# Five of nine down products of a mixture-of-experts slot go over to transposed, split products

## The chip, the cores and the metric

One core of a Trainium2 chip runs the whole program. The metric is the device time of one execution in microseconds (us), from the first to the last instruction with what lies around it; of several executions the median is taken.

## The reference

The input x is 16 batches of 512 tokens with 128 features, in float32. Six residual blocks run over it. The first three belong to the half of the program that the change touches (the front), the others to the back.

```
x = x + 0.5 * moe(layernorm(x));  x = x + attn0(layernorm(x));  x = x + 0.5 * moe(layernorm(x))
x = x + 0.5 * mlp(x normalised);  x = x + softmax_attention(x); x = x + 0.5 * mlp(...)

moe:  scores = sigmoid(x @ gate.T); top 2 of 16 experts, weights divided by their sum -> comb
      ye[e] = (silu(x @ We_gate[e]) * (x @ We_up[e])) @ We_down[e]     (16 experts, inner size 64)
      y = sum_e comb[:, e] * ye[e]  +  (silu(x @ Ws_gate) * (x @ Ws_up)) @ Ws_down  (inner size 128)
```

## The kernel before

The program has three parts one after another: `build_weights` (loads and splits the weights), `build_front`, `build_back`. The front works through **slots**. A slot is one `moe` of one batch (main work) with a share of other work beside it (side work): `SIDE = [ATT, MLP, ATT, MLP]`, so ATT slots carry the linear attention of another batch and MLP slots an `mlp`. There are 34 slots: one with no side work first, then 8 turns of 4, then one with no side work that also starts the back's first batch (`first_batch`). Each slot also prepares the next slot's input (`PREPARE` gives the tile index at which each step of this stands).

The 16 experts are taken in pairs, so a slot has NT = 9 tiles of 128 inner rows: tile 0 is the shared expert, 1 to 8 are pairs. For tile n, all with 512 tokens (T = 4 groups of 128):

- TensorE, `gate`: G = gate product, and U = up product. `product` makes a float32 product out of three passes with fp32r operands split in a high and a low part (wh*high + wl*high + wh*low), each pass one matmul of 512 columns.
- TensorE, `routing_weights`: C = comb weights spread over the rows of the tile, one matmul.
- ScalarE: s = silu(G) (L537).
- VectorE, `activated`: su = U * s (L691), and `routed`: h = C * su (L700), in three buffers h[n % 3].
- TensorE, `moe_down` with `down` (L861): Y[tokens, features] += h[:, t].T @ wd[n], four plain float32 matmuls of 128 columns. The trace records each of them twice, hence "x8".

At the end `main_residual` (VectorE, L704) adds 0.5 * Y to x.

Each engine has a program of its own, written out by hand in the order in which it runs; the engines meet through counting semaphores (`Signal`). TensorE's order within a slot, tile n: gate n, up n, C n, side work, main transposes (`PREPARE["transpose"]`), router logits, then `moe_down(n - 1)`. After tile 8 it runs the next slot's gate 0, and then `moe_down(8)`. G has two banks in PSUM, so gate n waits for the silu of tile n - 2. 

Side work on TensorE in an ATT slot: transposes of the side input zs (tile 2), `kvu_product` (tiles 3 and 4), `queries` (4), `keys_values` (5), `attend` (6). In an MLP slot: `out_transposes` (0), `wout` product (1), transposes (2), `hidden` (3 to 6), `mlp_down` (5 to 8).

GpSimd (POOL) runs, slot by slot: `side_start` (scale and offset of the side layernorm, and xb = x + bias), `main_normalise` (z of the next slot), and in ATT slots sin and cos products (kc, qc), uw and ub, `scale_offset` of the output norm, then og. It can't read PSUM. In the last slot it normalises the back's first batch (L463 to L475, result e_xn), which TensorE transposes at tile 4 (L958).

Of the kernel before, what the change touches and what calls it, by code (L numbers as in the profile page):

```python
# [19 lines left out]
F32R = mybir.dt.float32r  # L20
# [11 lines left out]
I_E = 64  # L32
TE = E * I_E // P
NT = TE + 1
FT = 4
GRP = 4
HG = H // GRP
# [19 lines left out]
class Chain:  # L57
# [36 lines left out]


PREPARE = {
    MLP: {"statistics": 2, "transpose": 4, "low": 4, "logits": 5, "scores": 6, "best": 6, "next": 7, "weights": 8},
    ATT: {"statistics": 1, "transpose": 3, "low": 3, "logits": 4, "scores": 5, "best": 6, "next": 7, "weights": 8},
}

# [71 lines left out]
def build_front(nc, weights, early, x_dram, mid_dram, ident_dram, staged_dram, tail_dram, turns):  # L172
    w = weights
    with ExitStack() as ctx:
# [50 lines left out]
        sbuf_s = [sb(f"s{p}", [P, T, P]) for p in range(2)]  # L225
        su = [sb(f"su{k}", [P, T, P]) for k in range(2)]
        h = [sb(f"h{k}", [P, T, P]) for k in range(3)]

        kvu = sb("kvu", [P, T, 3 * D])
        kc = sb("kc", [P, 2, T, D])  # L230
# [13 lines left out]

        hs = [sb(f"hs{k}", [P, T, P]) for k in range(2)]

        G = [ps(f"G{k}", [P, T, P]) for k in range(2)]
        U = ps("U", [P, T, P])
        C = ps("C", [P, T, P])
        Y = ps("Y", [P, T, P])  # L250
# [24 lines left out]
        weight_ready = sig("weight_ready", TE * NM, TE)  # L275
        h_ready = sig("h_ready", TE * NM, TE)
        down_done = sig("down_done", NT * NM, NT)

        main_done = sig("main_done", NM, 2)
        side_done = sig("side_done", NM, 1)  # L280
# [110 lines left out]
        def _(pool):  # L391
# [20 lines left out]
            def main_normalise(q, i):  # L412
# [5 lines left out]
                own.settle()  # L418
                nc.gpsimd.tensor_tensor(z[:], z[:], rstd[:].broadcast_to([P, T, D]), ALU.mult).then_inc(z_ready.sem, 1)

            def side_start(m, i, k):
                scale_offset(rstd_s, off_s, vpe_s, mv_s, smv_ready, smv_ready.at(i, k + 1), srstd_ready)

                pool.wait_ge(side_done.sem, side_done.at(i, k))
                bias = w["bout"] if SIDE[m] == ATT else w["b2h"]
                nc.gpsimd.tensor_tensor(xb[:], xw[SIDE_BATCH[m]][:], bias[:], ALU.add).then_inc(xb_ready.sem, 1)

            main_normalise(-1, 0)
            main_normalise(0, 0)

            own.step(nc.gpsimd.memset(early.va[:], 0.0))
            own.settle()
# [3 lines left out]
            for i in range(turns):  # L436
                for m in range(NM):
                    side_start(m, i, m)
                    main_normalise(m + 1, i)
                    if SIDE[m] == ATT:  # L440
                        a = nth(m)

                        pool.wait_ge(ka_ready.sem, ka_ready.at(i, a + 1))
                        nc.gpsimd.tensor_tensor(kc[:, 1], kvu[:, :, 0:D], w["sin_t"][:],
                                                ALU.mult).then_inc(ks_ready.sem, 1)

                        pool.wait_ge(qa_ready.sem, qa_ready.at(i, a + 1))
                        own.step(nc.gpsimd.tensor_tensor(qc[:, 0], qa[:], w["cos_c"][:], ALU.mult))
                        nc.gpsimd.tensor_tensor(qc[:, 1], qa[:], w["sin_c"][:], ALU.mult).then_inc(qc_ready.sem, 1)

                        pool.wait_ge(kvu_out.sem, kvu_out.at(i, T * (a + 1)))
                        own.step(nc.gpsimd.tensor_tensor(uw[:], kvu[:, :, 2 * D:], w["lnw"][:], ALU.mult))
                        own.step(nc.gpsimd.tensor_tensor(ub[:], kvu[:, :, 2 * D:], w["lnb"][:], ALU.mult))
                        scale_offset(rstd2, off2, vpe2, mv2, mv2_ready, mv2_ready.at(i, a + 1), rstd2_ready)

                        pool.wait_ge(on_ready.sem, on_ready.at(i, a + 1))
                        own.step(nc.gpsimd.tensor_tensor(og[:], on[:], uw[:], ALU.mult))
                        own.settle()
                        nc.gpsimd.tensor_tensor(og[:], og[:], ub[:], ALU.add).then_inc(og_ready.sem, 1)

            pool.wait_ge(early.mv_ready.sem, 1)
            _, mv_e, ve_e, rs_e = early.norm
            own.step(nc.gpsimd.tensor_tensor(ve_e[:], mv_e[:, :, 1], w["eps_two"][:], ALU.add))  # L463
# [9 lines left out]
            own.step(nc.gpsimd.tensor_tensor(early.xn[:], og[:], w["lns"][:], ALU.mult))  # L473
            own.settle()
            nc.gpsimd.tensor_tensor(early.xn[:], early.xn[:], w["lnsb"][:], ALU.add).then_inc(early.xn_ready.sem, 1)  # L475

        @block.scalar
        def _(act):
# [36 lines left out]
            def first_batch(n):  # L515
# [8 lines left out]
                if n == 8:  # L524
                    act.wait_ge(first_v.sem, 1)
                    nc.scalar.activation(store_values(early.va), values_in(Z), ACT.Copy)

            def slot(m, i, side, prepare):
                g0, steps = NT * m, PREPARE[side or MLP]
                for n in range(NT):  # L530
                    act.wait_ge(gate_ready.sem, gate_ready.at(i, g0 + n + 1))
                    if n >= 2:
                        act.wait_ge(up_used.sem, up_used.at(i, g0 + n - 1))
                    elif n == 0 and up_used.at(i, g0) > 0:

                        act.wait_ge(up_used.sem, up_used.at(i, g0))
                    nc.scalar.activation(sbuf_s[n % 2][:], G[n % 2][:], ACT.Silu).then_inc(act_done.sem, 1)  # L537
                    if n == 0:
                        act.wait_ge(combT_ready.sem, combT_ready.at(i, m + 1))
                        nc.scalar.activation(cT[m % 2][:], Z[:], ACT.Copy).then_inc(cT_ready.sem, 1)  # L540
                    if n == 0 and side == MLP:
                        act.wait_ge(oT_mm.sem, oT_mm.at(i, nth(m - 1) + 1))
                        nc.scalar.activation(oT[:], S[0][:], ACT.Copy).then_inc(oT_ready.sem, 1)
                    if n == 1 and side:
                        side_normalise(m, i, m)
                    if n == 2 and side:
                        side_high(i, m)
                    if prepare and n == steps["logits"] + 1:
                        scores(m + 1, i)
                    if side == ATT:  # L550
                        a = nth(m)
                        if n == 4:
                            act.wait_ge(kvu_out.sem, kvu_out.at(i, T * (a + 1)))
                            nc.scalar.activation(kvu[:, :, 0:D], kvu[:, :, 0:D], ACT.Silu).then_inc(ka_ready.sem, 1)
                            act.wait_ge(q_mm.sem, q_mm.at(i, a + 1))
                            nc.scalar.activation(qa[:], S[1][:], ACT.Silu, bias=w["bq"][:]).then_inc(qa_ready.sem, 1)
                        if n == 7:
                            out_normalise(a, i)
                    elif side == MLP:
                        if 3 <= n < 3 + FT:  # L560
                            hidden(m, n - 3, i)
                    if prepare:
                        if n == steps["transpose"]:
                            main_high(m + 1, i)
                        if n == steps["logits"]:
                            logits_half(m + 1, i)
                    else:
                        first_batch(n)

            main_high(-1, 0)  # L570
            logits_half(-1, 0)
# [8 lines left out]
        def _(dve):  # L580
# [112 lines left out]
            def routed(m, n, i):  # L693
# [1 line left out]
                g0, c0 = NT * m, TE * m  # L695
                dve.wait_ge(up_used.sem, up_used.at(i, g0 + n + 1))
                dve.wait_ge(weight_ready.sem, weight_ready.at(i, c0 + n))
                if n >= 3:
                    dve.wait_ge(down_done.sem, down_done.at(i, g0 + n - 2))
                nc.vector.tensor_tensor(h[n % 3][:], C[:], su[n % 2][:], ALU.mult).then_inc(h_ready.sem, 1)  # L700

# [130 lines left out]
        def _(pe):  # L832
# [30 lines left out]
                return mm  # L863

            def moe_down(m, n, i):
                if n == 0:

                    pe.wait_ge(main_done.sem, main_done.at(i, m))
                    pe.wait_ge(up_used.sem, up_used.at(i, NT * m + 1))
                else:  # L870
                    pe.wait_ge(h_ready.sem, h_ready.at(i, TE * m + n))
                down(Y, h[n % 3], w["wd"][:, n], n == 0).then_inc(down_done.sem, 1)

            def comb_transposes(m, i):
                if m < 0:
# [95 lines left out]

            def gate(m, n, i):
                g0 = NT * m
                if n >= 2:
                    pe.wait_ge(act_done.sem, act_done.at(i, g0 + n - 1))
                elif n == 0:
                    pe.wait_ge(xl_ready.sem, xl_ready.at(i, m + 1))
                    if m >= 0:

                        pe.wait_ge(act_done.sem, act_done.at(i, g0))  # L980
                product(G[n % 2], w["wgh"][:, n], w["wgl"][:, n], xh[m % 2], xl[m % 2]).then_inc(gate_ready.sem, 1)

            def slot(m, i, side, prepare):
                g0, a, steps = NT * m, nth(m), PREPARE[side or MLP]
                high, low = xh[m % 2], xl[m % 2]
                for n in range(NT):
# [34 lines left out]
                        logits(m + 1, i)  # L1021
                    if not prepare:
                        first_batch(n)
                    if n >= 1:
                        moe_down(m, n - 1, i)
                    if side == ATT:
                        if n == 2:
                            side_transposes(i, m)
# [3 lines left out]
                            keys_values(a, i)  # L1032
                if prepare:
                    gate(m + 1, 0, i)
                moe_down(m, NT - 1, i)

            main_transposes(-1, 0)
# [641 lines left out]
def build_weights(nc, front, back, a):  # L1679
# [24 lines left out]
    for name, (shape, _) in plain.items():  # L1704
        sb(name, shape)
    sb("wd", [P, NT, D])
    for name in ("minus_half", "eps", "eps_two", "both"):
        sb(name, [P, T])
    parts = {
# [18 lines left out]
    with ExitStack() as tmp:  # L1728
# [105 lines left out]
        def _(act):  # L1834
# [3 lines left out]
            for k, (whole, high, _) in enumerate(halves):  # L1838
                if k == first_others:
                    wait_loads(act, "others")  # L1840
                nc.scalar.activation(high, whole, ACT.Copy).then_inc(high_ready, 1)
            for n, f in enumerate(angle):
                act.wait_ge(angle_ready, n + 1)
                nc.scalar.activation(w[f + "_t"][:], angle[f][:], ACT.Sin).then_inc(table_ready, 1)
# [88 lines left out]
```

## Time and profile before

| | us |
|---|---|
| median of 3 runs | 1971.51 (1969.16 to 1973.76) |
| the profiled execution | 1970.83 |
| its span, first to last instruction | 1969.0 |
| TensorE busy in the span | 1879.2 (95%) |
| VectorE, ScalarE, GpSimd busy | 1533.5, 1167.0, 669.0 |

The front lasts to about 1146 us, with some 24 us of preparation ahead of it. "Busy" counts the time in which an instruction of the engine runs. Matmuls overlap each other in the records, so their cost is read from the distance between two starts, not from their length. In a timeline, a bracket at the end of a row is the engine's idle time before it and what ended that.

### The profile page before, as it was taken

The numbers are of one execution on the slowest core, as the hardware profiler recorded it, in microseconds if no ns is written. First come the engines' busy times: TensorE is split into PE (matmuls) and PEld (weight loads), VectorE is DVE, ScalarE is ACT, GpSimd is POOL, SyncE is SP. The second block draws the span as 40 slices with busy tenths as digits, with TensorE's granted clock in tenths as the row PEclk, the third lists the DMA queues.
The fourth block names the chain that finished last, engine by engine and source line by source line (L and its number), as shares of the span: only waits on it lengthen the run. The fifth ranks groups of instructions, "written<-read, shape, count | busy, mean of one in ns | idle before, by whom it ended". The sixth has DMA issues, their size and how long they took to land. (4 is left out here: it accounts for less than half of the span.)

```text
span 1969.0 us, 34154 instructions
## 1 busy us (share of the span) xinstructions
PE 1879.2 (95%) x12340; PEld 1296.4 (66%) x12340; DVE 1533.5 (78%) x3824; ACT 1167.0 (59%) x2178; POOL 669.0 (34%) x768
## 2 busy tenths in 40 slices
PE   2999999999999999999999989999999999999996
PEld 2888888888888888888888844444444444444433
DVE  5776767676767776777677669999999999999991
ACT  2444444444444444444444328888888888888885
POOL 2333433343334333433343323333333333333311
PEclk9999999999999999999999969999999999999998
DMA  3000000000000000000010022222222222222210
GB/s 133 7 12 1 12 11 12 1 12 12 11 1 11 12 12 1 12 12 11 1 38 6 6 86 87 87 87 87 90 94 91 91 92 92 92 88 87 86 46 11
DMA packets 49991, 85.81 MB, mean 44 GB/s; under 512 B 6752, under 2 KB 11104, under 8 KB 49760
## 3 DMA queue, kind: packets, MB, share of 16 engines
q1 hardware_dynamic: 47920, 81.85, 13.0%
q8 instruction: 99, 1.62, 0.3%
q10 hardware_dynamic: 1904, 1.78, 0.3%
q14 instruction: 68, 0.56, 0.1%
HBM read 49.26 MB, written 34.87 MB: 43 GB/s over the span
## 5 line engine op out<-in xcount | busy, mean ns | idle before, releaser
L1528 DVE TENSOR_REDUCE b_nm<-b_MX 128x1 f32<-128x512 f32 x1024 | 648.6, 682 | 46.0 <-PE b_MX L1636 31.2
L1420 ACT ACTIVATE b_pr<-b_ST 128x512 f32<-128x512 f32 x1024 | 550.2, 603 | 101.0 <-PE b_ST L1624 96.7
L537 ACT ACTIVATE s<-G 128x512 f32<-128x512 f32 x306 | 182.6, 597 | 294.6 <-PE G L856 290.3
L691 DVE TENSOR_TENSOR su<-U,s 128x512 f32<-128x512 f32 x272 | 187.0, 687 | 208.7 <-PE U L856 106.4
L861 PE MATMUL Y<-w_wd,h 128*128 128x128 f32 x2448 | 328.2, 277 | 4.3 <-DVE h L700 4.3
L861 PEld LDWEIGHTS Y<-w_wd,h 128*128 128x128 f32 x2448 | 308.8, 192 | 26.7 <-DVE h L700 14.7
L1636 PE MATMUL b_MX<-b_kt,b_qt 32*128 32x512 f32 x768 | 240.6, 504 | 2.2 <-DVE b_nm L1528 1.8
L1624 PE MATMUL b_ST<-b_qt,b_kt 32*128 32x512 f32 x768 | 213.9, 494 | 6.1 <-ACT b_pr L1420 6.1
L1624 PEld LDWEIGHTS b_ST<-b_qt,b_kt 32*128 32x128 f32 x768 | 83.3, 181 | 203.8 <-ACT b_pr L1420 135.9
L700 DVE TENSOR_TENSOR h<-C,su 128x512 f32<-128x512 f32 x272 | 188.0, 691 | 9.3
L854 PE MATMUL G<-xh,w_wgh 128*128 128x512 f32 x306 | 145.5, 475 | 0.0
L404 POOL TENSOR_TENSOR vpe_s<-mv_s,w_eps 128x4 f32<-128x4 f32 x32 | 6.4, 200 | 399.6 <-DVE mv_s L595 399.6
L1651 PE MATMUL b_PV<-b_pr,e_va 128*32 128x512 f32 x1024 | 139.0, 615 | 0.0
L1651 PE MATMUL b_PV<-b_pr,b_va 128*32 128x512 f32 x1024 | 136.4, 605 | 0.0
L854 PE MATMUL U<-xh,w_wuh 128*128 128x512 f32 x306 | 126.7, 414 | 1.2 <-DVE h L691 0.7
L856 PE MATMUL G<-xl,w_wgh 128*128 128x512 f32 x306 | 121.2, 396 | 0.0
L855 PE MATMUL G<-xh,w_wgl 128*128 128x512 f32 x306 | 121.0, 396 | 0.0
L856 PE MATMUL U<-xl,w_wuh 128*128 128x512 f32 x306 | 120.8, 395 | 0.0
L855 PE MATMUL U<-xh,w_wul 128*128 128x512 f32 x306 | 120.0, 392 | 0.0
L889 PE MATMUL C<-cT,w_pairs 128*128 128x512 f32 x272 | 107.7, 396 | 0.0
L1636 PEld LDWEIGHTS b_MX<-b_kt,b_qt 32*128 32x128 f32 x768 | 95.9, 185 | 15.9 <-DVE b_nm L1528 11.5
L494 ACT ACTIVATE zs<-xw,off_s,rstd_s 128x128 f32<-128x128 f32 x128 | 52.8, 483 | 66.6 <-POOL off_s L410 66.6
(295 smaller groups left out, 3629.7 us busy)
## 6 DMA issues: line engine op xcount, KB each, us to landing
b_kt<-staging SPq DMA_DIRECT2D x48, 256.0 KB, 2.7
b_qt<-staging SPq DMA_DIRECT2D x48, 256.0 KB, 3.0
staging<-e_khi SPq DMA_DIRECT2D x32, 256.0 KB, 2.9
staging<-e_qhi SPq DMA_DIRECT2D x32, 256.0 KB, 3.1
xin<-in_x SPq DMA_DIRECT2D x17, 256.0 KB, 2.8
mid<-xo SPq DMA_DIRECT2D x16, 256.0 KB, 2.0
staging<-e_klo SPq DMA_DIRECT2D x16, 256.0 KB, 3.0
staging<-e_qlo SPq DMA_DIRECT2D x16, 256.0 KB, 3.0
```

Of the source, the lines that this page charges most:

```text
L537: nc.scalar.activation(sbuf_s[n % 2][:], G[n % 2][:], ACT.Silu).then_inc(act_done.sem, 1)
L691: nc.vector.tensor_tensor(out[:], U[:], sbuf_s[n % 2][:], ALU.mult).then_inc(up_used.sem, 1)
L700: nc.vector.tensor_tensor(h[n % 3][:], C[:], su[n % 2][:], ALU.mult).then_inc(h_ready.sem, 1)
L854: pe.matmul(flat(bank), wh, flat(high), start=True, stop=False)
L855: pe.matmul(flat(bank), wl, flat(high), start=False, stop=False)
L856: return pe.matmul(flat(bank), wh, flat(low), start=False, stop=True)
L861: mm = pe.matmul(bank[:, t], hid[:, t], wd, start=(first and t == 0), stop=True, skip_group_check=True)
L1420: nc.scalar.activation(pr[k % 2][:, j], bank[:].rearrange("p a b -> p (a b)"), ACT.Exp, scale=SM_SCALE).then_inc(used["st"].sem, 1)
L1528: nc.vector.tensor_reduce(nm[g % 2][:, c:c + 1], bank[:].rearrange("p a b -> p (a b)"), AX.X, ALU.max).then_inc(used["mx"].sem, 1)
L1624: pe.matmul(flat(bank_of(B, "st", 0, u)), kt_[g][rows_of(j), k % T], flat(qt[g])[rows_of(j)], start=True, stop=True).then_inc(made["st"].s ...
L1636: pe.matmul(flat(bank_of(B, "mx", rel, u)), qt[g][rows_of(j), u // HG % T], flat(kt_[g])[rows_of(j)], start=True, stop=True).then_inc(made ...
L1651: mm = pe.matmul(flat(PV)[rows_of(j)], values_of(va[B.parity], kt, g, j), pr[k % 2][:, j], start=(k % (PAIR * T) == 0), stop=((k + 1) % (P ...
```

## The change

Tiles 2 to 6 (`V0, NV = 2, 5`) of each slot get another down product. ScalarE copies h to hh (fp32r, the high part), GpSimd makes hl = h - hh (the low part), and TensorE adds three passes of 512 columns, wdh*hh + wdl*hh + wdh*hl, to a bank V that holds the sum transposed (features x tokens). At the end of the slot ScalarE copies V to vs and TensorE adds its transposes to Y. V takes the place of the second G bank, so gate n now waits for the silu of tile n - 1. The down products of tiles 2 to 6 stand one tile later on TensorE (`moe_down(n - 2)`), so tile 3 has none, and tile 8 has those of tiles 6 and 7. The main statistics in MLP slots go from tile 2 to tile 1, GpSimd's xb goes behind `main_normalise`, and the weights wdh and wdl are made once.

```diff
+V0, NV = 2, 5
 PREPARE = {
-    MLP: {"statistics": 2, "transpose": 4, ...
+    MLP: {"statistics": 1, "transpose": 4, ...
...
+        hh = [sb(f"hh{k}", [P, T, P], F32R) for k in range(3)]
+        hl = [sb(f"hl{k}", [P, T, P], F32R) for k in range(3)]
+        vs = sb("vs", [P, T, P])
-        G = [ps(f"G{k}", [P, T, P]) for k in range(2)]
+        G = ps("G", [P, T, P])
+        V = ps("V", [P, T, P])
...  GpSimd
+            def low(m, n, i):
+                pool.wait_ge(hh_ready.sem, hh_ready.at(i, NV * m + n - V0 + 1))
+                nc.gpsimd.tensor_tensor(hl[n % 3][:], h[n % 3][:], hh[n % 3][:],
+                                        ALU.subtract).then_inc(hl_ready.sem, 1)
...
             main_normalise(-1, 0)
+            own.step(nc.gpsimd.tensor_tensor(w["wdl"][:], w["wd"][:, V0:V0 + NV], w["wdh"][:], ALU.subtract))
+            own.settle()
             main_normalise(0, 0)
+            lows(-1, 0, range(V0, V0 + NV))
...
                     side_start(m, i, m)
-                    main_normalise(m + 1, i)
-                    if SIDE[m] == ATT:
+                    if SIDE[m] == MLP:
+                        main_normalise(m + 1, i)
+                        lows(m, i, (2,))
+                        side_bias(m, i, m)
+                        lows(m, i, (3, 4, 5, 6))
+                    else:
                         a = nth(m)
+                        main_normalise(m + 1, i)
+                        lows(m, i, (2,))
+                        side_bias(m, i, m)
+                        lows(m, i, (3,))
...  (kc, then qc)
+                        lows(m, i, (4,))
...  (uw, ub)
+                        lows(m, i, (5,))
                         scale_offset(rstd2, off2, vpe2, mv2, mv2_ready, mv2_ready.at(i, a + 1), rstd2_ready)
+                        lows(m, i, (6,))
...  (og)
+            lows(0, turns, (2, 3))
             pool.wait_ge(early.mv_ready.sem, 1)
...  (e_xn)
+            lows(0, turns, (4, 5, 6))
...  ScalarE
+            def high(m, n, i):
+                act.wait_ge(h_ready.sem, h_ready.at(i, TE * m + n))
+                nc.scalar.activation(hh[n % 3][:], h[n % 3][:], ACT.Copy).then_inc(hh_ready.sem, 1)
+            def down_copy(m, i):
+                act.wait_ge(down_done.sem, down_done.at(i, NT * m + V0 + NV))
+                nc.scalar.activation(vs[:], V[:], ACT.Copy).then_inc(vs_ready.sem, 1)
...  (slot, behind the silu of tile n; down_copy at the slot's end)
+                    if V0 < n <= V0 + NV:
+                        high(m, n - 1, i)
...  VectorE, routed
-                if n >= 3:
+                if n >= V0 + 3:
+                    dve.wait_ge(hl_ready.sem, hl_ready.at(i, NV * m + n - V0 - 2))
+                elif n >= 3:
                     dve.wait_ge(down_done.sem, down_done.at(i, g0 + n - 2))
...  TensorE, moe_down
+                k = n - V0
+                if 0 <= k < NV:
+                    high, low = hh[n % 3], hl[n % 3]
+                    pe.wait_ge(hh_ready.sem, hh_ready.at(i, NV * m + k + 1))
+                    pe.matmul(flat(V), w["wdh"][:, k], flat(high), start=(k == 0), stop=False, skip_group_check=True)
+                    pe.wait_ge(hl_ready.sem, hl_ready.at(i, NV * m + k + 1))
+                    pe.matmul(flat(V), w["wdl"][:, k], flat(high), start=False, stop=False, skip_group_check=True)
+                    pe.matmul(flat(V), w["wdh"][:, k], flat(low), start=False, stop=True,
+                              skip_group_check=True).then_inc(down_done.sem, 1)
+                    return
...
+            def down_transposes(m, i):
+                pe.wait_ge(vs_ready.sem, vs_ready.at(i, m + 1))
+                for t in range(T):
+                    pe.matmul(Y[:, t], vs[:, t], w["ident"][:], start=False, stop=True, is_transpose=True,
+                              skip_group_check=True)
...  gate
-                if n >= 2:
-                    pe.wait_ge(act_done.sem, act_done.at(i, g0 + n - 1))
+                if n >= 1:
+                    pe.wait_ge(act_done.sem, act_done.at(i, g0 + n))
...  slot
-                    if n >= 1:
+                    if 1 <= n <= V0:
                         moe_down(m, n - 1, i)
+                    if n >= V0 + 2:
+                        moe_down(m, n - 2, i)
+                    if n == NT - 1:
+                        moe_down(m, NT - 2, i)
...
                 if prepare:
                     gate(m + 1, 0, i)
+                down_transposes(m, i)
                 moe_down(m, NT - 1, i)
...  build_weights, ScalarE, ahead of the sine tables
+            wait_loads(act, "down")
+            nc.scalar.activation(w["wdh"][:], w["wd"][:, V0:V0 + NV], ACT.Copy)
```

## Rows read from the trace of the kernel before

**Rows 1.** Busy time by engine in two stretches: start:end, length, engines, granted clock, DMA.
```profile
300.00:500.00 200.00, 197.28 (x1257) 172.16 (x1256) 144.68 (x434) 89.47 (x156) 70.48 (x89) 1.00 0.03 9
1148.00:1150.00 2.00, 0.80 (x3) 0.29 (x3) 0.00 (x0) 0.00 (x0) 1.86 (x4) 0.50 0.82 255
```

**Rows 2.** Timeline of TensorE, ATT slot: start us, length us, engine, line, operation, tiles.
```profile
409.07 0.60 PE L839 MATMUL Z<-w_ident,z 128*128 128x128 f32 x4
409.51 1.06 PE L861 MATMUL Y<-w_wd,h 128*128 128x128 f32 x8
410.32 0.48 PE L854 MATMUL G<-xh,w_wgh 128*128 128x512 f32 x1
...
411.10 0.40 PE L854 MATMUL U<-xh,w_wuh 128*128 128x512 f32 x1
...
411.79 0.40 PE L889 MATMUL C<-cT,w_pairs 128*128 128x512 f32 x1
...
413.88 1.14 PE L861 MATMUL Y<-w_wd,h 128*128 128x128 f32 x8
414.77 0.48 PE L854 MATMUL S<-xhs,w_wqh 128*128 128x512 f32 x1
...
421.46 1.95 PE L944 MATMUL S<-kvm,qc 128*128 128x128 f32 x16
...
430.25 1.16 PE L861 MATMUL Y<-w_wd,h 128*128 128x128 f32 x8 [0.22 <-DVE h L700]
...
431.16 0.48 PE L854 MATMUL U<-xh,w_wuh 128*128 128x512 f32 x1
```

**Rows 3.** Timeline of TensorE, the MLP slot that follows.
```profile
445.38 0.66 PE L839 MATMUL Z<-w_ident,z 128*128 128x128 f32 x4 [0.22 <-POOL z L419]
...
459.21 0.48 PE L854 MATMUL G<-xh,w_wgh 128*128 128x512 f32 x1
...
464.22 0.47 PE L854 MATMUL U<-xh,w_wuh 128*128 128x512 f32 x1
```

**Rows 4.** Timeline of TensorE, the first and the last slot of the front.
```profile
56.36 0.66 PE L839 MATMUL Z<-w_ident,z 128*128 128x128 f32 x4 [1.13 <-POOL z L419]
...
1130.12 0.60 PE L958 MATMUL Z<-w_ident,e_xn 128*128 128x128 f32 x4
...
1149.03 0.80 PE L1636 MATMUL b_MX<-e_kt,e_qt 32*128 32x512 f32 x3 [3.01 <-DMA e_qt<-staging]
```

**Rows 5.** Timeline of ScalarE: preparation, ATT slot, MLP slot.
```profile
21.14 0.63 ACT L1844 ACTIVATE w_cos_t<-t_angle_cos 128x512 f32<-128x512 f32 x1 [5.26 <-DVE t_angle_cos L1826]
...
405.24 0.57 ACT L537 ACTIVATE s<-G 128x512 f32<-128x512 f32 x1
...
418.35 0.26 ACT L490 ACTIVATE en<-lg 128x64 f32<-128x64 f32 x1
...
426.75 1.51 ACT L494 ACTIVATE on<-S,off,rstd 128x128 f32<-128x128 f32 x4 [1.12 <-POOL off L410]
...
457.20 0.60 ACT L537 ACTIVATE s<-G 128x512 f32<-128x512 f32 x1
```

**Rows 6.** Timeline of GpSimd: ATT slot, then last slot of the front.
```profile
415.14 1.80 POOL L444 TENSOR_TENSOR kc<-kvu,w_sin_t 128x512 f32<-128x512 f32 x1 [6.72 <-ACT kvu L554]
...
424.83 0.20 POOL L404 TENSOR_TENSOR vpe<-mv,w_eps 128x4 f32<-128x4 f32 x1 [2.92 <-DVE mv L595]
...
429.69 1.27 POOL L459 TENSOR_TENSOR og<-og,ub 128x512 f32<-128x512 f32 x1
...
1120.99 0.20 POOL L463 TENSOR_TENSOR e_ve<-e_mv,w_eps_two 128x4 f32<-128x4 f32 x1 [21.11 <-DVE e_mv L595]
...
1126.23 1.30 POOL L475 TENSOR_TENSOR e_xn<-e_xn,w_lnsb 128x512 f32<-128x512 f32 x1
```

**Rows 7.** Timeline of VectorE, ATT slot.
```profile
418.64 0.82 DVE L628 TENSOR_SCALAR en<-en 128x64 f32<-128x64 f32 x1
...
430.11 0.93 DVE L669 TENSOR_TENSOR first<-first,second 128x64 f32<-128x64 f32 x1
```

More of the change, by code:

```diff
@@ L96 @@
 PREPARE = {
-    MLP: {"statistics": 2, "transpose": 4, "low": 4, "logits": 5, "scores": 6, "best": 6, "next": 7, "weights": 8},
+    MLP: {"statistics": 1, "transpose": 4, "low": 4, "logits": 5, "scores": 6, "best": 6, "next": 7, "weights": 8},
     ATT: {"statistics": 1, "transpose": 3, "low": 3, "logits": 4, "scores": 5, "best": 6, "next": 7, "weights": 8},
@@ L277, in build_front @@
         down_done = sig("down_done", NT * NM, NT)
+        hh_ready = sig("hh_ready", NV * NM, NV)
+        hl_ready = sig("hl_ready", NV * NM, NV)
+        vs_ready = sig("vs_ready", NM, 1)
         main_done = sig("main_done", NM, 2)
@@ L419, in main_normalise, with lows, side_bias @@
                 nc.gpsimd.tensor_tensor(z[:], z[:], rstd[:].broadcast_to([P, T, D]), ALU.mult).then_inc(z_ready.sem, 1)
+            def low(m, n, i):
+                pool.wait_ge(hh_ready.sem, hh_ready.at(i, NV * m + n - V0 + 1))
+                nc.gpsimd.tensor_tensor(hl[n % 3][:], h[n % 3][:], hh[n % 3][:],
+                                        ALU.subtract).then_inc(hl_ready.sem, 1)
+            def lows(m, i, tiles):
+                for n in tiles:
+                    low(m, n, i)
             def side_start(m, i, k):
                 scale_offset(rstd_s, off_s, vpe_s, mv_s, smv_ready, smv_ready.at(i, k + 1), srstd_ready)
+            def side_bias(m, i, k):
                 pool.wait_ge(side_done.sem, side_done.at(i, k))
@@ L536, in slot @@
                         act.wait_ge(up_used.sem, up_used.at(i, g0))
-                    nc.scalar.activation(sbuf_s[n % 2][:], G[n % 2][:], ACT.Silu).then_inc(act_done.sem, 1)
+                    nc.scalar.activation(sbuf_s[n % 2][:], G[:], ACT.Silu).then_inc(act_done.sem, 1)
                     if n == 0:
@@ L568, in slot @@
                         first_batch(n)
+                down_copy(m, i)
             main_high(-1, 0)
@@ L973, in gate @@
                 g0 = NT * m
[L974 to L976 removed]
+                if n >= 1:
+                    pe.wait_ge(act_done.sem, act_done.at(i, g0 + n))
+                else:
                     pe.wait_ge(xl_ready.sem, xl_ready.at(i, m + 1))
@@ L980, in gate @@
                         pe.wait_ge(act_done.sem, act_done.at(i, g0))
-                product(G[n % 2], w["wgh"][:, n], w["wgl"][:, n], xh[m % 2], xl[m % 2]).then_inc(gate_ready.sem, 1)
+                product(G, w["wgh"][:, n], w["wgl"][:, n], xh[m % 2], xl[m % 2]).then_inc(gate_ready.sem, 1)
             def slot(m, i, side, prepare):
@@ L1706, in build_weights @@
     sb("wd", [P, NT, D])
+    sb("wdh", [P, NV, D], F32R)
+    sb("wdl", [P, NV, D], F32R)
     for name in ("minus_half", "eps", "eps_two", "both"):
```

## The prediction

> **What bounds the kernel now.** I looked first at the busy time in stretches. In the middle of the front TensorE is busy for 197 of 200 us, with the clock granted in full; VectorE has 145, ScalarE 89, GpSimd 70 [rows 1]. So work taken off TensorE counts nearly in full, as long as the slower engines keep up. Next the timeline of TensorE, where costs are distances between starts. An old down product takes 0.81 (409.51 to 410.32), and the gate pass behind it starts a product of 0.78 (410.32 to 411.10) where the up product of the same form takes 0.69 (411.10 to 411.79). So the change from float32 to fp32r costs 0.08 or 0.09, and a down costs 0.89 all told, as in 413.88 to 414.77 [rows 2]. A three-pass product is what the new down will be: 0.70. Four transposes cost 0.44 (409.07 to 409.51) [rows 2]. Last, the brackets: in the slots shown TensorE waits 0.22 for h of tile 8 at 430.25 and 0.22 for z at 445.38, and in the first slot 1.13 for z [rows 2 to 4].
>
> **The change, TensorE's work.** Each slot loses five downs of 0.89, and 0.08 more at tile 4 of ATT (tile 5 of MLP), where the down stands between two fp32r groups: 4.53. It gains five products of 0.70 and one group of transposes, 3.50 + 0.44 = 3.94. That is 0.59 a slot less, 20 us over 34 slots.
>
> **ATT slots.** I follow the trace of before with only the changed steps moved. Tile 3 has no down, and the later products are shorter, so TensorE could reach `attend` 1.25 earlier than 421.46: 0.89 from tile 3, 0.27 at tile 4, and 0.19 at tile 5, less some 0.1 that the wait for xls ahead takes. ScalarE however must do high(4) (0.60, as any copy of 128x512; a silu is 0.57 to 0.60 [rows 5]) ahead of the table load for the router scores, so en comes at 418.1 instead of 418.35, only 0.25 earlier. VectorE runs four score steps behind en and then the mask of the heads that `attend` needs, and one of them is likely held by a GpSimd operation, below. I get the mask at 420.4 and `attend` at 420.5: 0.95 early, a new wait of 0.3.
> From the end of `attend` to the next slot's up product TensorE now needs 7.9 (431.16 less 421.46 + 1.78). After: product 4 0.78, two times gate, up and C 3.26, products 5 and 6 1.40, the down of tile 7 0.81, gate 0 0.78, transposes 0.44, the down of tile 8 0.89, sum 8.4; the down that no longer stands at tile 3 comes back here, and the wait of 0.22 goes. Product 6 needs GpSimd's low(6), which stands behind `scale_offset`. That begins at 424.83 and hands over at 426.7, where ScalarE's `on` starts [rows 5, 6]. Both come 0.8 earlier, at 425.9; low(6) costs 1.3 (og, a product of the same size, is 1.27 [rows 6]) and ends at 427.2, and TensorE asks at 427.2 to 427.3. I charge 0.1. The gain of an ATT slot is 0.95 - 0.5, about 0.5.
>
> **MLP slots.** GpSimd has nothing but z, xb and the low parts, and each low part is there a microsecond or more ahead of its product. The statistics at tile 1 fall into VectorE's idle time while ScalarE waits for the side norm, z comes 3 us earlier, and the wait of 0.22 goes. Gate 8 needs the silu of tile 7 (457.20), which stands behind high(5) and two table loads; I get 456.4 for it and 457.2 for gate 8 (before 459.21 [rows 3, 5]), a slack of 0.8. The product at the end waits for nothing. Gain 0.59 + 0.22, and 0.1 for places where two float32 groups come together: 0.9.
>
> **One bank for G.** Gate n is held by the silu of tile n - 1. The tightest place is gate 3 of ATT: silu 2 ends at 405.8 [rows 5] and gate 3 can start then, as before. A wait for xls stands behind it and hides a slip of 0.2. Cost 0, bound 0.4 a slot.
>
> **The ends.** First slot: 0.59 and the wait of 1.13 for z, 1.7. Preparation: the copy of wd stands ahead of the sine tables, where ScalarE later waits 5.26 for VectorE's cosine angles [rows 5], so 0; if the load were late it could cost 2. GpSimd makes wdl while it is idle.
> Last slot: here the change adds a wait that has no cover. GpSimd does low(2) and low(3) first and then normalises the back's first batch. That chain takes 6.5 (1120.99 to 1127.5 [rows 6]), and before it was over 2.6 ahead of its transposes at 1130.12 [rows 4]. Low(3) needs high(3), which needs silu 4 and with it gate 4, at the very tile where TensorE waits for the result. In the slot's old times: gate 4 ends at 1128.3, silu, high and low bring 1131.1, the chain 1137.6. TensorE stands from 1129.3 to 1137.7, and the transposes are 7.6 later than before. The keys and queries of the first batch, their staging and the back's first matmul (1149.03 [rows 4]) all hang on these transposes. After an idle time of 3 us the clock was granted at 0.50, the lower level, at the start of the back [rows 1, 4], so I add 2 for products at 1.2 GHz after the stall: 9.5 lost (bounds 7 and 12).
>
> **Sum.** 16 x 0.5 + 16 x 0.9 + 1.7 - 9.5 = 14.6. The profiled execution is 1970.8, which gives 1956.2; the median of the runs is 0.7 higher: 1957.
>
> **GpSimd and VectorE.** Two rows of before show that they hold each other up. VectorE's en + 1 takes 0.82 and its first + second 0.93, with GpSimd in a product of two SBUF tiles that ends at that moment (og runs from 429.69 to 430.96, first + second from 430.11 to 431.04); GpSimd's kc takes 1.80 instead of 1.27 beside VectorE's own kc product [rows 6, 7]. The low parts add five GpSimd operations of this kind to a slot, and about 20 small VectorE operations of the router lie among them.
> The Trainium skill ("SBUF — State Buffer", Who interferes with whom) says that an operation with two SBUF inputs on VectorE contends with a GpSimd instruction that reads SBUF, and that the second to issue fully blocks until the first has finished. The trace agrees, with the 0.93 above. By that rule every small operation that meets a low part waits up to 1.3; it is the rule that speaks most against the change, and rival D is what it could do.
>
> **Rivals.**
> B, all waits are covered: the mask and low(6) come in time, and an ATT slot gains its full 0.59 and the idle 0.3. For it: my two waits are each a few tenths and come out of small shifts. Against: both chains pass through two engines that are now busier. Price 16 x 0.4 = 6.4 better: 1950.
> C, the silu comes late: the single bank of G, with ScalarE's queue lengthened by five copies, holds a gate by 0.8 in each MLP slot beyond my slack (the place is gate 8 behind the two table loads). For it: silu 7 is the latest silu of before. Against: 0.8 of slack. Price 16 x 0.8 = 13: 1970.
> D, slower: low parts take 1.80 as kc does, since VectorE's two-input operations hold them. Three stand ahead of the output norm and product 6 in an ATT slot (4, 5 and 6), 0.5 each, so product 6 and the silu of tile 8 come 1.5 late: 16 x 1.5 = 24, 1981. It makes the kernel slower than before from 0.9 lost a slot (14.6 / 16). For it: the slack at product 6 is nil. Against: uw and ub run in the same stretch at about 1.3 undisturbed.
> That the new product is not cheaper than the old one is not among them, because gate and up have its exact form.
>
> **How the numbers follow.** About 0.2% (4 us) is what a measurement of this kernel can tell from no change. Chances: forecast (1952 to 1963) 0.50, B 0.17, C 0.20 (1963 to 1975, half of it faster by over 0.2%), D 0.13. Faster 0.77, same 0.10, slower 0.13. The range takes in B with some room, and C up to 1972; D and the rest stay out: 1946 to 1972.
>
> **What would show it.** Starts of new products 0.70 apart from what follows; in ATT slots TensorE waiting some tenths ahead of `attend` for VectorE (kvm) and hardly for hl; an idle TensorE of about 8.4 us ahead of the e_xn transposes in the last slot, with a granted clock of 0.50 behind it; slots in the middle shorter by 0.5 and 0.9. Wrong would be: brackets with hl or hh on many rows, brackets with s at gates, low parts of 1.8, or a last slot without the wait.

## The result, and the profile after

The changed kernel takes 1959.65 us (1958.95 to 1959.95, 4 runs) against 1971.69 of the kernel before, a ratio of 0.9939 with a 95% interval of 0.9922 to 0.9956. Forecast were 1957 and "faster". The profiled execution has a span of 1957.2.

From the page of the kernel after, the engines' busy times and the groups of the low and the high parts:

```profile
PE 1860.5 (95%) x11626; PEld 1258.0 (64%) x11626; DVE 1553.3 (79%) x3824; ACT 1272.9 (65%) x2383; POOL 886.6 (45%) x939
...
L432 POOL TENSOR_TENSOR hl<-h,hh 128x512 fp32r<-128x512 f32 x170 | 219.3, 1290 | 180.6 <-ACT hh L565 180.6
...
L565 ACT ACTIVATE hh<-h 128x512 fp32r<-128x512 f32 x170 | 105.9, 623 | 0.0
```

GpSimd's low part takes 1.29 on average over 170 of them (not the 1.8 of rival D), and ScalarE's high part 0.62. Ahead of the low parts GpSimd sat idle for 180 us in all, waiting for hh.

The busy times in the middle of the front, and then stretches of the last slot. The third figure from the end is the granted clock, as a share of the full one:

```profile
300.00:500.00 200.00, 197.42 (x1149) 168.42 (x1148) 150.27 (x433) 111.84 (x200) 113.86 (x124) 1.00 0.03 9
...
1112.00:1114.00 2.00, 0.00 (x0) 0.00 (x0) 0.00 (x0) 0.00 (x0) 1.92 (x2) 0.70 0.00 0
1116.00:1118.00 2.00, 2.00 (x8) 1.71 (x7) 0.53 (x1) 0.60 (x1) 0.00 (x0) 0.50 0.00 0
1118.00:1120.00 2.00, 2.00 (x7) 1.57 (x6) 0.17 (x1) 0.59 (x2) 0.00 (x0) 0.60 0.00 0
1120.00:1122.00 2.00, 2.00 (x11) 1.61 (x10) 1.38 (x2) 0.63 (x3) 1.29 (x1) 1.00 0.01 4
```

TensorE is as busy as before (197.4 of 200, [rows 1]); VectorE went from 145 to 150, ScalarE from 89 to 112, GpSimd from 70 to 114.

The best yardstick is the distance from one slot's first up product to the next one's. It is steady to some hundredths of a us within a kind of slot, so a single profile gives it. The means over 16 slots of a kind, with the first slot, the stretch from the last slot's up product to the back's first matmul, and the rest:

| | before | after | change | forecast |
|---|---|---|---|---|
| ATT slot | 32.40 | 32.33 | -0.07 | -0.5 |
| MLP slot | 33.05 | 31.83 | -1.22 | -0.9 |
| first slot | 34.26 | 32.21 | -2.05 | -1.7 |
| last slot, to the back | 30.29 | 38.91 | +8.62 | +9.5 |
| ahead of the first up product | 37.24 | 38.12 | +0.88 | 0 |
| back | 819.97 | 821.41 | +1.44 | 0 |

In sum 16 x (0.07 + 1.22) = 20.6 and 2.05 gained, 8.62 + 0.88 + 1.44 = 10.9 lost: 11.8, the difference of the spans. The last two lines are scatter. Over eleven profiles (both kernels and the nine experiments below) the preparation ends between 36.1 and 39.9, without order between kernels that share it, and the back lasts 818.3 to 822.1.

The total is 2.6 us from the forecast, but two terms of it were off by 7 and 5 us in opposite directions, and that they nearly cancelled was luck. So the experiments ask first where an ATT slot's gain went.

**An ATT slot after.** TensorE, the slot that starts at 391.18 and ends at 423.51:

```profile
391.18 0.48 PE L903 MATMUL U<-xh,w_wuh 128*128 128x512 f32 x1
...
412.75 2.02 PE L1010 MATMUL S<-kvm,qc 128*128 128x128 f32 x16
414.53 0.48 PE L919 MATMUL V<-hh,w_wdh 128*128 128x512 f32 x1
...
419.27 0.40 PE L919 MATMUL V<-hh,w_wdh 128*128 128x512 f32 x1
...
419.99 1.05 PE L910 MATMUL Y<-w_wd,h 128*128 128x128 f32 x8
...
421.58 0.60 PE L937 MATMUL Y<-w_ident,vs 128*128 128x128 f32 x4
422.60 1.16 PE L910 MATMUL Y<-w_wd,h 128*128 128x128 f32 x8 [0.41 <-DVE h L749]
423.51 0.48 PE L903 MATMUL U<-xh,w_wuh 128*128 128x512 f32 x1
```

`attend` stands 21.57 after the slot's start, and 22.70 in the slot of [rows 2] (421.46, its start being 431.16 less 32.40): 1.13 gained up to there. From the row behind `attend` to the end it takes 8.98 (414.53 to 423.51), and 7.92 before, from this row to 431.16:

```profile
423.24 1.06 PE L861 MATMUL Y<-w_wd,h 128*128 128x128 f32 x8
```

Product 6 (419.27 to 419.99) shows no wait for its low part. The transposes start at 421.58 and need 0.44, but the down of tile 8 starts at 422.60: 0.58 lost to h.

VectorE, GpSimd and ScalarE at that place:

```profile
417.90 0.69 DVE L749 TENSOR_TENSOR h<-C,su 128x512 f32<-128x512 f32 x1
418.51 0.93 DVE L699 TENSOR_TENSOR hit<-rest,m 128x64 f32<-128x64 f32 x1
...
419.99 1.09 DVE L710 TENSOR_TENSOR second<-hit,r 128x64 f32<-128x64 f32 x1
...
421.14 0.68 DVE L738 TENSOR_TENSOR su<-U,s 128x512 f32<-128x512 f32 x1
```

```profile
406.68 1.80 POOL L474 TENSOR_TENSOR kc<-kvu,w_sin_t 128x512 f32<-128x512 f32 x1 [1.36 <-ACT kvu L600]
...
418.06 1.29 POOL L432 TENSOR_TENSOR hl<-h,hh 128x512 fp32r<-128x512 f32 x1
419.72 1.28 POOL L490 TENSOR_TENSOR og<-on,uw 128x512 f32<-128x512 f32 x1 [0.36 <-ACT on L529]
```

```profile
410.21 0.26 ACT L525 ACTIVATE en<-lg 128x64 f32<-128x64 f32 x1
...
419.52 0.61 ACT L581 ACTIVATE s<-G 128x512 f32<-128x512 f32 x1
```

VectorE is done with h of tile 7 at 418.5 and goes on with the router's step `next`. Its first operation (L699) takes 0.93 instead of 0.22, and ends as low(6) ends (418.06 + 1.29 = 419.35). By then `next` is 0.7 late, and its `second` (L710) starts inside og, which began at 419.72: it takes 1.09, until og ends at 421.0. Only then comes su of tile 8, at 421.14, although s was there at 420.1. The rows of [rows 7] had one such hold in this place of the slot, on the step behind h of tile 8 (L669), where hardly anything waited for it.

**An MLP slot after.** TensorE, the transposes of z in the slot that starts at 1065.06:

```profile
1077.78 0.60 PE L888 MATMUL Z<-w_ident,z 128*128 128x128 f32 x4
```

They have no bracket any more, and stand 12.72 after the slot's start, against 14.22 in [rows 3] (445.38 less 431.16).

**The last slot after.** TensorE, then GpSimd:

```profile
1107.31 0.43 PE L955 MATMUL C<-cT,w_pairs 128*128 128x512 f32 x1
1115.69 1.11 PE L1024 MATMUL Z<-w_ident,e_xn 128*128 128x128 f32 x4 [7.96 <-POOL e_xn L509]
1116.46 0.78 PE L919 MATMUL V<-hh,w_wdh 128*128 128x512 f32 x1
...
1135.79 0.50 PE L1707 MATMUL b_MX<-e_kt,e_qt 32*128 32x512 f32 x3 [2.71 <-DMA e_qt<-staging]
```

```profile
1107.92 1.26 POOL L432 TENSOR_TENSOR hl<-h,hh 128x512 fp32r<-128x512 f32 x1 [0.43 <-ACT hh L565]
1109.14 0.20 POOL L497 TENSOR_TENSOR e_ve<-e_mv,w_eps_two 128x4 f32<-128x4 f32 x1
...
1114.38 1.26 POOL L509 TENSOR_TENSOR e_xn<-e_xn,w_lnsb 128x512 f32<-128x512 f32 x1
```

Low(3) runs from 1107.92 and the chain of the early norm right behind it, until 1115.64. TensorE waits 7.96. The transposes stand 18.81 after the last slot's up product (1096.88), 11.38 before: 7.43 late, where 7.6 were forecast. TensorE had stood idle since the C product of 1107.31. The granted clock was 0.70 in 1112:1114 (a mean of its upper level and the lower one, 1.2 GHz), 0.50 in 1116:1118, with TensorE at work again since 1115.69, and 1.00 from 1120 on. From the transposes to product 2 it takes 0.77 there (1115.69 to 1116.46), and 0.35 at full clock in `early_norm_first` below.

### The profile page after: what moved, and what is told of

Read it like the earlier page. It is cut to its first block and busy times, and to the rows that moved or that the text cites. A ratio compares the mean times of both kernels' runs of the same rounds, so it can differ in the third digit from the quotient of the medians.

```text
span 1957.2 us, 33103 instructions
## 1 busy us (share of the span) xinstructions
PE 1860.5 (95%) x11626; PEld 1258.0 (64%) x11626; DVE 1553.3 (79%) x3824; ACT 1272.9 (65%) x2383; POOL 886.6 (45%) x939
## 5 line engine op out<-in xcount | busy, mean ns | idle before, releaser
L432 POOL TENSOR_TENSOR hl<-h,hh 128x512 fp32r<-128x512 f32 x170 | 219.3, 1290 | 180.6 <-ACT hh L565 180.6
L910 PE MATMUL Y<-w_wd,h 128*128 128x128 f32 x1088 | 145.3, 276 | 6.7 <-DVE h L749 6.7
L910 PEld LDWEIGHTS Y<-w_wd,h 128*128 128x128 f32 x1088 | 137.7, 192 | 16.8 <-DVE h L749 10.5
L903 PE MATMUL G<-xh,w_wgh 128*128 128x512 f32 x306 | 136.0, 444 | 0.7 <-ACT s L581 0.7
L565 ACT ACTIVATE hh<-h 128x512 fp32r<-128x512 f32 x170 | 105.9, 623 | 0.0
```

The source lines that it names most:

```text
L432: nc.gpsimd.tensor_tensor(hl[n % 3][:], h[n % 3][:], hh[n % 3][:], ALU.subtract).then_inc(hl_ready.sem, 1)
L903: pe.matmul(flat(bank), wh, flat(high), start=True, stop=False)
L910: mm = pe.matmul(bank[:, t], hid[:, t], wd, start=(first and t == 0), stop=True, skip_group_check=True)
```

## The experiments

All edits are to the kernel after, if nothing else is said. "Slot" is the distance from above.

### early_norm_first: the back's norm ahead of the low parts

```diff
-            lows(0, turns, (2, 3))
             pool.wait_ge(early.mv_ready.sem, 1)
...
-            lows(0, turns, (4, 5, 6))
+            lows(0, turns, (2, 3, 4, 5, 6))
```

> The changed kernel with one move on GpSimd in the last slot of the front: the norm of the back's first batch (e_xn) runs ahead of low(2) and low(3). Theory: the wait of 7.96 us ahead of the e_xn transposes comes only from that order, and with the clock at half speed behind it the last slot lost 8.6 us; so the stretch from the last up product 0 to the back's first matmul falls from 38.9 to about 29.7 us (30.3 in the kernel before, less 0.6 of TensorE work), and the time to about 1950.5 us. Rival: ScalarE and GpSimd are too full in that slot whatever the order, and most of the wait comes back at product 2 or 3, waiting for hl; then the stretch stays above 34 us and the time above 1955.

Measured: 1949.13 us (1948.05 to 1951.02), ratio to the kernel before 0.9883 (0.9869 to 0.9898). The last stretch is 28.88 us, down from 38.91; slots as in after (32.32, 31.80). TensorE, last slot:

```profile
1107.98 0.43 PE L954 MATMUL C<-cT,w_pairs 128*128 128x512 f32 x1
1108.25 0.60 PE L1023 MATMUL Z<-w_ident,e_xn 128*128 128x128 f32 x4
1108.60 0.48 PE L918 MATMUL V<-hh,w_wdh 128*128 128x512 f32 x1
```

The transposes follow C at once and none of the later products waits. The order of GpSimd's program was the whole loss: it is worth 10.0 us in that stretch, 0.8 more than expected, since a wait of 0.45 for h of tile 8 in the kernel before (at 1144.86) is gone as well, and the wait for the DMA ahead of the back is 0.3 shorter.

### att_next_earlier: the router's `next` at tile 6

```diff
-    ATT: {..., "best": 6, "next": 7, "weights": 8},
+    ATT: {..., "best": 6, "next": 6, "weights": 8},
```

> The changed kernel with the router's step 'next' on VectorE in ATT slots one tile earlier (tile 6 instead of 7), where GpSimd runs only tiny operations. Theory: an ATT slot is 32.33 us long, 0.5 longer than its TensorE work, because VectorE's two-input operations there are held by GpSimd's low(6) (0.93 instead of 0.2) and then by og (1.09), so h of tile 8 comes 0.6 late (wait of 0.41 at the down of tile 8). Then the ATT slot falls to about 31.9 us, the wait at tile 8 goes, and the time falls by 6 us to about 1953.5. Rival: ScalarE's queue (high(6), then the output norm, then silu 8) sets h of tile 8; then VectorE waits for s instead, the slot stays at 32.3 and the time at 1959.5.

Measured: 1979.33 us (1977.25 to 1981.16), ratio to before 1.0039 (1.0024 to 1.0053): slower than both kernels. ATT slot 33.60, MLP slot 31.83. The theory and the rival both failed, and the trace says why. VectorE, GpSimd, and TensorE's wait:

```profile
422.96 0.23 DVE L710 TENSOR_TENSOR second<-hit,r 128x64 f32<-128x64 f32 x1
423.10 1.28 DVE L712 TENSOR_TENSOR share<-sc,den 128x64 f32<-128x64 f32 x1
424.31 0.68 DVE L738 TENSOR_TENSOR su<-U,s 128x512 f32<-128x512 f32 x1
```

```profile
423.01 1.29 POOL L432 TENSOR_TENSOR hl<-h,hh 128x512 fp32r<-128x512 f32 x1
```

```profile
425.05 0.49 PE L903 MATMUL U<-xh,w_wuh 128*128 128x512 f32 x1 [1.69 <-DVE su L738]
```

The step ran free of holds up to its last operation. That one (share, L712) started 0.09 behind low(6) and was held for the whole of it, 1.28 instead of 0.22, and behind it on VectorE stood su of tile 7, which frees U: TensorE waits 1.69 for it (26.8 us over the 16 slots). The place of a hold matters more than its number: in after, two holds of together 1.6 cost 0.58; here one of 1.1 made the slot 1.3 longer than in after.

### low6_memset: a low(6) that reads nothing

```diff
-                        lows(m, i, (6,))
+                        pool.wait_ge(hh_ready.sem, hh_ready.at(i, NV * m + 6 - V0 + 1))
+                        nc.gpsimd.memset(hl[0][:].bitcast(F32), 0.0).then_inc(hl_ready.sem, 1)
```

> The changed kernel with the low part of tile 6 in ATT slots left out: GpSimd fills hl with zeros instead (it writes SBUF and reads nothing), so the product of tile 6 lacks the share of its low part in these slots. Theory that GpSimd's reads hold VectorE: the hit step of 'next' takes 0.2 instead of 0.93, 'next' is over before og starts, so its 'second' step takes 0.2 instead of 1.09, the wait of 0.41 for h of tile 8 goes, and the ATT slot falls from 32.33 to about 31.75 us; time about 1950. Rival (ScalarE's queue sets h of tile 8): slot at 32.2 or more.

Measured: 1946.34 us in one run; ATT slot 31.60, MLP slot 31.82. VectorE, and GpSimd beside it:

```profile
416.10 0.21 DVE L700 TENSOR_TENSOR hit<-rest,m 128x64 f32<-128x64 f32 x1
...
416.86 0.23 DVE L711 TENSOR_TENSOR second<-hit,r 128x64 f32<-128x64 f32 x1
...
417.74 0.69 DVE L739 TENSOR_TENSOR su<-U,s 128x512 f32<-128x512 f32 x1 [0.52 <-ACT s L582]
```

```profile
415.62 0.53 POOL L488 MEMSET hl<- 128x512 f32 x1
417.31 1.28 POOL L491 TENSOR_TENSOR og<-on,uw 128x512 f32<-128x512 f32 x1 [1.16 <-ACT on L530]
```

`hit` takes 0.21 and `second` 0.23; `next` is over before og begins, and su of tile 8 waits for s, not for VectorE. The slot is 0.73 shorter: with low(6) both holds go. (The next one in line, on the step behind h of tile 8, comes back as it was before the change, at 0.95, and again hardly anything waits for it.) But the memset is also shorter than low(6), 0.53, and ends at 416.15, when `hit` had just begun. So this run doesn't tell whether the reading of low(6) holds VectorE or only its length. That needs a long operation that only writes.

### low6_memset_long: a second memset behind the first

```diff
                         nc.gpsimd.memset(hl[0][:].bitcast(F32), 0.0).then_inc(hl_ready.sem, 1)
+                        nc.gpsimd.memset(pad[:], 0.0)
```

(Against low6_memset; `pad` is 128x1024.)

> low6_memset with a second memset of GpSimd behind the first, of 128x1024 into a tile that nothing reads, so that GpSimd only writes from 415.6 to about 417.2 (estimate: 2 x 0.53 more). (As in low6_memset the low part of tile 6 is left out in ATT slots: zeros take its place.) VectorE's next step (hit to share, eight operations from 416.1 to 417.0) then lies wholly inside a GpSimd operation. Theory: VectorE is held by a GpSimd operation that reads SBUF, not by one that only writes: every operation of the step keeps its 0.15 to 0.23, and the ATT slot stays at 31.60 (31.5 to 31.7). Rival: any long GpSimd operation holds it, and low6_memset escaped because its memset ended 0.05 after hit had begun: second or one of the operations behind hit then takes about 1 us (until 417.2), the step ends 0.3 to 1 later, and the ATT slot is up to 0.4 longer, 31.7 to 32.0. In both MLP slot 31.82, total 1943 to 1950.

Measured: 1957.57 us in one run; ATT slot 32.18, MLP slot 31.81. Neither forecast had this. VectorE, and GpSimd beside it:

```profile
419.41 0.23 DVE L705 TENSOR_TENSOR hit<-hit,w_ramp 128x64 f32<-128x64 f32 x1
419.55 0.58 DVE L707 TENSOR_SCALAR den<-den 128x4 f32<-128x4 f32 x1
...
420.38 1.35 DVE L715 TENSOR_TENSOR share<-sc,den 128x64 f32<-128x64 f32 x1
421.65 0.68 DVE L741 TENSOR_TENSOR su<-U,s 128x512 f32<-128x512 f32 x1
```

```profile
419.15 0.95 POOL L490 MEMSET pad<- 128x1024 f32 x1
420.37 1.28 POOL L493 TENSOR_TENSOR og<-on,uw 128x512 f32<-128x512 f32 x1 [0.26 <-ACT on L532]
```

The 2-input operation L705 (`hit` times the ramp) lies wholly inside the memset and takes 0.23: not held, as my theory had it. But the tensor_scalar behind it (L707, 128x4, one input) is held until the memset ends, 0.58 instead of 0.16, in each of the 16 ATT slots. I had not told the two kinds apart. The Trainium skill does ("SBUF — State Buffer", Who interferes with whom): a VectorE instruction with two SBUF inputs contends with a GpSimd instruction that reads SBUF and not with one that only writes it, while a tensor_scalar can enter a 2-port mode, in which it contends with GpSimd. This trace agrees with both, by the 0.23 and the 0.58.

What follows is worth more. The hold of 0.42 alone should cost nothing, since VectorE waited 0.52 for s in low6_memset. But it made `share` (L715) start 0.01 behind og, which held it for 1.35, and su starts at 421.65. So the slot is 0.58 longer than in low6_memset, by a first hold of another cause than in the kernel after. A delay of some 0.4 that pushes `next` into og is all that it takes.

### stats_back_at_2: the early statistics undone

```diff
-    MLP: {"statistics": 1, ...
+    MLP: {"statistics": 2, ...
```

> The changed kernel with the main statistics in MLP slots and in the first slot back at tile 2. Theory: the MLP slot's gain of 1.22 us, more than the 0.59 of TensorE work plus the old wait of 0.22, leans on z being there early: TensorE now asks for z 1.3 us earlier than before, so at tile 2 the statistics cost a wait of about 1.3 us for z, and 0.5 more since low(2) stands behind z; MLP slot 31.83 to about 33.3 us, first slot 2 us longer, time about 1984. Rival: the early statistics only remove the old wait of 0.22; MLP slot about 32.1 us, time about 1965.

Measured: 1994.03 us in one run. MLP slot 33.78 (1.95 more than after), first slot 36.27, ATT slot 32.34. TensorE, an MLP slot:

```profile
449.36 0.66 PE L888 MATMUL Z<-w_ident,z 128*128 128x128 f32 x4 [1.13 <-POOL z L427]
...
450.59 0.50 PE L921 MATMUL V<-hh,w_wdl 128*128 128x512 f32 x1 [0.34 <-POOL hl L432]
```

The mechanism is the one forecast, z first and low(2) behind it, and it is larger: 2.0 a slot instead of 1.5, 4 instead of 2 in the first slot. (There the wait for z is 1.89, and the granted clock was 0.50 for some 3 us behind it.) Without this one digit the change would have made the kernel 22 us slower.

### before_one_bank: the kernel before with one bank for G

```diff
-        G = [ps(f"G{k}", [P, T, P]) for k in range(2)]
+        G = ps("G", [P, T, P])
...
-                if n >= 2:
-                    pe.wait_ge(act_done.sem, act_done.at(i, g0 + n - 1))
+                if n >= 1:
+                    pe.wait_ge(act_done.sem, act_done.at(i, g0 + n))
```

> The kernel before with the one bank for G alone (gate n waits for the silu of tile n - 1), nothing else changed. Theory: every silu is over before TensorE comes to the next gate, so both kinds of slot stay as long as before (ATT 32.40, MLP 33.05 us, within 0.05) and the time stays at 1971. Rival C of the prediction (the silu comes late, above all behind the two table loads): MLP or ATT slots 0.4 to 0.8 longer, time 1978 to 1984.

Measured: 1972.92 us in one run (before, on the same chip, 1973.1); slots 32.40, 33.04, first slot 34.28, each within 0.02 of the kernel before. The bank alone costs nothing. This run lacks the five high parts that lengthen ScalarE's queue; for these the trace of after has to answer (below, rival C).

### before_early_stats: the kernel before with the statistics at tile 1

```diff
-    MLP: {"statistics": 2, ...
+    MLP: {"statistics": 1, ...
```

> The kernel before with the main statistics of MLP slots and of the first slot at tile 1 instead of 2, nothing else changed. Theory: the gap of 0.38 us ahead of the z transposes goes in MLP slots (33.05 to 32.67 us) and 1.5 us in the first slot, time about 1963.5: about half a percent comes from this part without the new products. Rival: VectorE is late for something else at tile 1 and gives it back; MLP slot 33.0 or more, time 1970.

Measured: 1965.95 us in one run. MLP slot 32.62 (0.43 less), first slot 32.96 (1.30 less), ATT slot 32.40. The slots are near the theory; the time is 2.5 above it, as much as this profile's preparation (39.72) is longer than that of before. So 16 x 0.43 + 1.30 = 8.2 us of the change's gain come without any new product.

### att_four_tiles: early_norm_first, and no low(6) in ATT slots

```diff
+def tiles_v(m, i):
+    return NV - 1 if m >= 0 and SIDE[m] == ATT and i < NB // 2 else NV
...
-                        lows(m, i, (6,))
...
-                if 0 <= k < NV:
+                if 0 <= k < tiles_v(m, i):
```

(The counts of the semaphores follow, and the copy of V waits for tile 5 in these slots.)

> early_norm_first, and in ATT slots tile 6 keeps the old float32 down product, so GpSimd makes no low(6) there. Theory (GpSimd's reads hold VectorE's router step): TensorE does 0.19 us more in an ATT slot, but the wait for h of tile 8 and the delay that VectorE passes on go; ATT slot 32.32 to about 31.8 us, MLP slot 31.80 as in early_norm_first, time 1949 to about 1941. Rival (the zeros in low6_memset gained by being shorter, or by freeing TensorE of its wait for hl): ATT slot 32.3 or longer by the 0.19, time 1949 to 1952.

Measured: 1940.55 us (1939.53 to 1941.81), ratio to before 0.9839 (0.9823 to 0.9856). ATT slot 31.83, MLP slot 31.81. TensorE at the slot's end, and VectorE's `next`:

```profile
418.95 0.60 PE L945 MATMUL Y<-w_ident,vs 128*128 128x128 f32 x4
419.39 1.06 PE L918 MATMUL Y<-w_wd,h 128*128 128x128 f32 x8
```

```profile
415.70 0.22 DVE L707 TENSOR_TENSOR hit<-rest,m 128x64 f32<-128x64 f32 x1
...
416.46 0.23 DVE L718 TENSOR_TENSOR second<-hit,r 128x64 f32<-128x64 f32 x1
```

The down of tile 8 follows the transposes after 0.44: no wait. One new product less, and the slot is 0.49 shorter.

### all_four_tiles: early_norm_first with NV = 4

```diff
-V0, NV = 2, 5
+V0, NV = 2, 4
```

> early_norm_first with four new products in every slot (NV = 4, tiles 2 to 5) instead of five. Theory: ATT slot about 31.8 us as in att_four_tiles, MLP slot 31.80 plus the 0.19 that one old down costs over a new product, 31.99; time about 1944. Rival (each new product is worth more than 0.19 since the low part's path counts too, or less since its cover is nil): MLP slot outside 31.9 to 32.1.

Measured: 1943.08 us (1942.45 to 1946.26), ratio 0.9853 (0.9838 to 0.9868). ATT slot 31.81, MLP slot 32.01: 0.21 more than with five products. That is the price difference of one old and one new product, in slots that otherwise run alike; the prediction had 0.89 - 0.70 = 0.19. (Its first slot is 34.59 long, 1.8 more than in `att_four_tiles`. A GpSimd memset of 1.38 held VectorE's en + 1, a tensor_scalar, for 1.14, where it took 0.20 in `att_four_tiles`, and TensorE waited 1.31 instead of 0.35 for su. Behind that wait the granted clock was 0.50 in 66:68, and the two downs of tiles 6 and 7 took 3.07 there, 1.70 in the MLP slots.)

## Why the prediction was right, and where it was not

**TensorE's work** was right: 0.59 a slot rests on 0.19 for each product, where all_four_tiles shows 0.21, and on 0.44 for the transposes, which att_four_tiles shows again.

**MLP slots**: 1.22 gained, 0.9 forecast. The term that was too small is the wait for z. I took the bracket of 0.22 at 445.38 [rows 3], but the transposes could have started 0.38 earlier than they did (before_early_stats gains 0.43 from this part alone). In a bracket the pipeline's overlap is already taken off; the distance between starts is the price. The rest, 1.22 - 0.43 = 0.79, is the 0.59 and about 0.2 at the slot's head, where TensorE waits less for the router's weights and for the side norm (its transposes stand 6.75 after the slot's start, 6.95 before). This part was not in my sum at all.

**ATT slots**: 0.07 gained, 0.5 forecast; the step that failed is the one from `attend` to the end. Up to `attend` I had 0.95 and it was 1.13 (en came at 410.21, 19.03 after the slot's start, against 19.59 in [rows 5]: 0.56 earlier, not 0.25). Behind it I charged 0.5 and it was 1.06. I followed low(6) only to TensorE's product 6, charging 0.1 there, and it does come in time. I had the rule that a small VectorE operation that meets a low part waits up to 1.3, but did not follow VectorE's own chain, from `next` to su and h of tile 8, through the new schedule. There low(6) holds the step once, and, pushed back by 0.7, the step then runs into og, which it had escaped before. low6_memset and att_four_tiles show that low(6) starts this: without it both holds are gone, and the slot falls to 31.60 and 31.83. low6_memset_long shows that the second hold is enough for most of the cost: with a first hold of only 0.42, from a memset, `next` runs into og and the slot is at 32.18. ScalarE's queue, the rival, is ruled out by low6_memset, where ScalarE still makes the high part of tile 6 and the gain is there all the same.

**The last slot**: the added wait without cover was right in place and size, 7.43 late against 7.6, and 8.62 in all against 9.5. early_norm_first shows that the order was its cause; it even ends 1.4 below the old 30.29. From the transposes to the back's first matmul it takes 18.91 before, 20.10 after and 18.18 in early_norm_first at full clock: the lower clock cost about 1.9 (2 forecast), and the 0.7 that the slot gains there was not in the sum.

**The ends**: right in sum. First slot 2.05 against 1.7. I gave the preparation 0 with a bound of 2; its scatter between profiles is larger than any effect that I could tell.

**The rivals.** B (all waits covered) didn't happen in ATT slots, and it is what att_four_tiles makes come true: 1940.6 with the last slot mended. C (the silu comes late) did not happen in the 32 slots with side work: no gate there waits for s, in after or in before_one_bank. At C's own place, gate 8 of the MLP slot that starts at 423.51, silu 7 ends at 448.24 and the gate starts at 449.26, a slack of 1.0. Only gate 8 of the first slot waits for it:

```profile
64.40 0.50 PE L903 MATMUL G<-xh,w_wgh 128*128 128x512 f32 x1 [0.73 <-ACT s L581]
```

D rests on the rule of the Trainium skill that the prediction cites ("SBUF — State Buffer", Who interferes with whom), and put its price on the wrong side: GpSimd's low parts stay at 1.29, since it was VectorE that came second. At product 6 there was no wait for hl, and the holds cost 0.58 on VectorE instead of 1.5 on GpSimd. D's stretched 1.80 stayed where it was, on kc (406.68), with VectorE's kc begun just ahead of it (406.64).

The prediction calls the trace of before in agreement with that rule, and this is so for the holds that it names. But the same trace has two-input operations that were not held: `first` at 425.15 (0.23) and `rest` at 425.42 (0.22) ran inside GpSimd's power for rstd, a tensor_tensor of 128x4 that reads SBUF and lasts 1.01 from 425.11. It is the same in all 16 ATT slots. There the measurement decides: not every GpSimd instruction that reads SBUF holds VectorE for its whole length.

## What to carry to other kernels

When work is added to an engine that shares something with another, follow the other engine's instructions through the new schedule, one by one, up to the next instruction that somebody waits for: a hold of 1 us on a 0.2 us operation costs next to nothing in one place and makes a slot 1.3 longer in the next. Look for the one-off stretches of a program (its last turn, a hand-over) when a block is inserted into a loop; here one such place took back 8.6 us of a gain of 22.7. And take the price of a wait from the distance between starts, not from the idle time in its bracket.

## What the runs showed of the hardware

- A VectorE operation of 128x64 with two SBUF inputs that takes 0.22 alone took 0.93, 1.09 and 1.28 when it started inside a GpSimd operation of 1.3 that reads SBUF, each time until that ended. The start decides: 0.09 late was enough for 1.28, and 0.01 for 1.35. With VectorE first it was GpSimd that took longer: kc 1.80 instead of 1.27, begun 0.04 behind VectorE's kc.
- Inside GpSimd's power of 128x4, which reads SBUF too and lasts 1.02, such operations kept their 0.22 to 0.23 (32 of 32 in after).
- Inside a GpSimd memset of 0.95 such an operation took 0.23, but a tensor_scalar of 128x4 with one input was held to the memset's end (0.58 instead of 0.16).
- A whole slot of some 180 matmuls repeats to a few hundredths of a us from turn to turn and from run to run (MLP slot 31.80 to 31.83 in six kernels that share it), while the stretch ahead of it, which waits for loads, scatters by 4 us (and the first slot by 1). Slot lengths of one profile tell more than the total time of several runs.
